# A conditional adapter with layer norm and a per-sample projection: transposes moved from TensorE to VectorE and DMA

## The reference

```python
h = relu(x @ W1[id0] + b1)                 # 512 -> 128
a = x + (h @ W2[id0] + b2)                 # 128 -> 512
n = (a - mean(a)) * rsqrt(var(a) + 1e-5)   # over the 512 columns
x1 = x + n * gamma + beta
out = x1 + (x1 @ W[id1] + b)               # 512 -> 512
```

## Time and profile before

| what | value |
|---|---|
| median of 3 runs (lowest, highest) | 313.99 us (313.78, 314.19) |
| span of the profiled execution | 312.3 us |
| PE busy | 303.9 us (97%) |
| DVE, ACT, POOL busy | 225.6, 211.1, 225.8 us (72%, 68%, 72%) |
| TensorE clock granted | 1.00 of full speed in every slice |
| DMA packets, volume | 40943 packets, 65.39 MB |

### The profile page before, as it was taken

One profiled execution on the slowest core, in us unless ns is written; L12 is line 12 of the kernel. 1 busy time (PEld: TensorE's weight loads), 2 busy tenths in 40 slices (PEclk: granted clock), 3 DMA queues, 4 the chain that ended last, 5 costly groups with the idle time before them and its releaser, 6 DMA issues.

```text
span 312.3 us, 4810 instructions
## 1 busy us (share of the span) xinstructions
PE 303.9 (97%) x1424; PEld 244.4 (78%) x1424; DVE 225.6 (72%) x641; ACT 211.1 (68%) x381; POOL 225.8 (72%) x185
## 2 busy tenths in 40 slices
PE   8988999999999999999999999999999999999995
PEld 8424678888888888888888888888888888888884
DVE  0185989696986869598686969778695977889610
ACT  1045667886696958778596857958686874857431
POOL 0649685999779995999959996899959995541000
PEclk9999999999999999999999999999999999999999
DMA  6999795778766798768867888677867381111122
GB/s 199 338 364 370 237 338 176 218 233 284 216 172 212 207 297 250 182 185 258 275 192 197 232 256 247 154 215 246 303 202 198 111 300 37 67 67 71 67 101 101
DMA packets 40943, 65.39 MB, mean 209 GB/s; under 512 B 6100, under 2 KB 10196, under 8 KB 40916
## 3 DMA queue, kind: packets, MB, share of 16 engines
q1 hardware_dynamic: 40336, 64.03, 66.2%
q10 hardware_dynamic: 580, 1.05, 1.1%
HBM read 48.29 MB, written 16.78 MB: 208 GB/s over the span
## 4 chain that ended last, share of the span: by engine, by line
PE 92%; DVE 4%; ACT 2%; issue 1%; POOL 0%; POOLq 0%
PE out_ps L778 54%; PE down_ps L778 14%; PE h_ps L778 13%; PE turn_ps L833 9%; PE turn_ps L904 2%; DVE y L488 1%; ACT y L376 1%; DVE stats L493 1%; DVE turn_ps L532 0%; DVE x1T_lo L539 0%; ACT w_hi L347 0%; ACT hT L358 0%; ACT out_sb L394 0%; DVE mean_var L497 0%; ACT w_hi L341 0%
## 5 line engine op out<-in xcount | busy, mean ns | idle before, releaser
L778 PE MATMUL out_ps<-x1T_hi,w_hi 128*128 128x512 f32 x256 | 100.4, 392 | 0.0
L778 PE MATMUL out_ps<-x1T_lo,w_hi 128*128 128x512 f32 x256 | 99.8, 390 | 0.0
L778 PE MATMUL out_ps<-x1T_hi,w_lo 128*128 128x512 f32 x256 | 99.7, 389 | 0.0
L687 POOL TENSOR_TENSOR xrow<-xrow,b_rows 128x512 f32<-128x512 f32 x64 | 82.6, 1294 | 9.3 <-DMA xrow<-x_rows 9.3
L385 ACT ACTIVATE x1T_hi<-turn_ps,gamma_beta 128x512 fp32r<-128x512 f32 x64 | 43.2, 689 | 43.7 <-DVE turn_ps L532 43.7
L532 DVE SCALAR_TENSOR_TENSOR turn_ps<-turn_ps,gamma_beta,xT 128x512 f32<-128x512 f32 x64 | 45.4, 754 | 34.4 <-PE turn_ps L833 33.5
L376 ACT ACTIVATE y<-y,shift,rstd 128x512 f32<-128x512 f32 x64 | 52.2, 818 | 20.4 <-DVE shift L523 20.0
L692 POOL TENSOR_TENSOR xT_lo<-xT,xT_hi 128x512 fp32r<-128x512 f32 x48 | 62.4, 1300 | 4.7 <-ACT xT_hi L328 4.7
L488 DVE TENSOR_TENSOR y<-down_ps,xrow 128x512 f32<-128x512 f32 x64 | 43.7, 683 | 19.6 <-PE down_ps L778 19.5
L778 PEld LDWEIGHTS out_ps<-x1T_hi,w_hi 128*128 128x128 f32 x256 | 48.1, 188 | 10.9 <-issue 0.8
L778 PEld LDWEIGHTS out_ps<-x1T_hi,w_lo 128*128 128x128 f32 x256 | 48.1, 188 | 10.1 <-issue 0.2
(11 more groups left out here) (40 smaller groups left out, 356.8 us busy)
## 6 DMA issues: line engine op xcount, KB each, us to landing
xrow<-x_rows SPq DMA_DIRECT2D x32, 512.0 KB, 6.7
out_cols<-out_sb SPq DMA_DIRECT2D x64, 256.0 KB, 2.6
xT<-x_cols SPq DMA_DIRECT2D x30, 512.0 KB, 6.2
w<-w_all SPq DMA_DIRECT2D x8, 1024.0 KB, 7.2
w<-w_all SPq DMA_DIRECT2D x15, 256.0 KB, 5.2
b_rows<-b_all SPq DMA_DIRECT2D x8, 256.0 KB, 8.1
xT<-x_cols ACTq DMA_DIRECT2D x4, 256.0 KB, 4.6
w<-w_all SPq DMA_DIRECT2D x4, 64.0 KB, 3.7
```

The source lines that it names most:

```text
L687: nc.gpsimd.tensor_tensor(xrow[:, i % XR, :], xrow[:, i % XR, :], b2_rows[:, m % 2, :], ALU.add).then_inc(rowbias_done, 1)
L778: mm = nc.tensor.matmul(out, lhsT, rhs, start=first and n == 0, stop=last and n == len(terms) - 1)
```

## The change

From tile 8 on (block 2; `SQUARED` is 8) `turn` is gone. In its place `square(i)` on VectorE transposes each 32x32 square of a normalised tile into an SBUF tensor `squares`, and `move(blk)` copies these to their places in `normT` by 16 DMAs of 64 KB a block, in rows of 512 bytes, eight issued by SP and eight by ScalarE. `merge` reads `normT` instead of PSUM. For this the rows of a block are loaded in another order (row 4p+t of the block in partition p of tile t), and `relu` writes its block in that order.

From tile 11 on (`POWER`) GpSimd takes the inverse root as a power (`inverse_root`), after an `add_eps` on VectorE; `standard` and the Newton step are gone there. `up` is one float32 product for every tile, so `x_hi`, `x_lo`, `w1_high` and `w1_low` are gone. Merges come two steps later (s modulo 4 is 3 or 0), `out(s)` becomes `out(s-9)` with steps 13 and 15 left without one, `finish` and `store` follow it, and the columns are loaded 8 tiles ahead instead of 10.

```diff
-    LOAD_COLS, LOAD_ROWS = 10, 6
-    OUT = -7
+    LOAD_COLS, LOAD_ROWS = 8, 6
+    OUT = -9
+    SQUARED = 2 * BLOCK
+    POWER = OPEN = 11
+    def merged(s):
+        first = {3: s - 7, 0: s - 6}.get(s % BLOCK, -1)
+        return (first, first + 1) if first >= SQUARED and there(first) else ()
+    def out_of(s):
+        i = {7: 0, 8: 1, 9: 2, 10: 3, 11: 4, 12: 5, 13: -1, 14: 6, 15: -1, 16: 7}.get(s, s + OUT)
+        return i if there(i) else None
+    def moved(s):
+        blk = (s - 5) // BLOCK
+        return blk if s % BLOCK == 1 and SQUARED <= blk * BLOCK < TILES else None
...
+            def move(blk):                                   # ScalarE; SP has range(2)
+                act.wait_ge(square_done, BLOCK * (blk + 1) - SQUARED)
+                act.wait_ge(merge_done, BLOCK * blk)
+                for q in range(2, KC):
+                    for j in range(KC):
+                        source = squares[Q * q:Q * (q + 1), blk % 2].rearrange("a (k j) r -> a k j r", j=KC)[:, :, j, :]
+                        nc.scalar.dma_start(normT[Q * j:Q * (j + 1), :, q * P:(q + 1) * P], source
+                                            ).then_inc(moved_in[q], 16)
...
             def step(s):                                     # ScalarE
+                if out_of(s - 1) is not None:
+                    finish(out_of(s - 1))
+                if moved(s) is not None:
+                    move(moved(s))
+                if there(s + NORM):
+                    normalise(s + NORM)
                 if (s + UP) % BLOCK == BLOCK - 1 and there(s + UP):
                     relu((s + UP) // BLOCK)
+                for i in merged(s):
+                    x1_high(i)
                 if (s + UP) % BLOCK == BLOCK - 1 and there(s + UP):
                     h_high((s + UP) // BLOCK)
...
+            def square(i):                                   # VectorE
+                blk, t = i // BLOCK, i % BLOCK
+                dve.wait_ge(norm_done, i + 1)
+                nc.vector.transpose(squares[:, blk % 2, :, t::BLOCK], y[:, i % WR, :]).then_inc(square_done, 1)
             def step(s):                                     # VectorE
+                if there(normed):
+                    mean_shift(normed)
+                if there(new):
+                    add_rows(new)
+                if first is not None:
+                    merge(first)
+                if there(new):
+                    statistics(new)
+                if second is not None:
+                    merge(second)
+                if there(new):
+                    mean_variance(new)
+                if first is not None:
+                    x1_low(first)
+                if there(new):
+                    add_eps(new)
+                if second is not None:
+                    x1_low(second)
+                if there(normed):
+                    square(normed)
...
+            def inverse_root(i):                             # GpSimd, last in its step(s)
+                pool.wait_ge(vareps_done, i - POWER + 1)
+                nc.gpsimd.tensor_tensor(rstd[:, r], var_eps[:, r], neg_half[:], ALU.pow).then_inc(rstd_done, 1)
...
-                for i in turned(s):                          # TensorE
-                    turn(i)
                 if there(s + DOWN):
                     down(s + DOWN)
                 if there(s + UP):
                     up(s + UP)
```

More of the change, by code:

```diff
@@ L84, in cond_resid_kernel @@
         y = sb("y", [P, WR, D])
+        squares = sb("squares", [P, 2, D // Q, P])
+        normT = sb("normT", [P, KC, NB])
         x1T_hi = sb("x1T_hi", [P, WR, NB], f32r)
@@ L136, in cond_resid_kernel @@
         up_done, down_done, turn_done, out_done = (sem(n) for n in ("up_done", "down_done", "turn_done", "out_done"))
-        xhi_done, xlo_done = sem("xhi_done"), sem("xlo_done")
+        square_done = sem("square_done")
+        moved_in = [sem(f"moved_in{q}") for q in range(KC)]
         relu_done, hhi_done, hlo_done = sem("relu_done"), sem("hhi_done"), sem("hlo_done")
@@ L241, in load_rows @@
                     sp.wait_ge(y_done, i + 2 - XR)
-                sp.dma_start(xrow[:, i % XR:i % XR + 2, :],
-                             x_rows[i * P:(i + 2) * P, :].rearrange("(t p) d -> p t d", p=P)
-                             ).then_inc(rows_in[i // 2 % (XR // 2)], 16)
+                if i < SQUARED:
+                    rows = x_rows[i * P:(i + 2) * P, :].rearrange("(t p) d -> p t d", p=P)
+                else:
+                    first, t = i - i % BLOCK, i % BLOCK
+                    rows = x_rows[first * P:first * P + NB, :].rearrange("(p t) d -> p t d", t=BLOCK)[:, t:t + 2, :]
+                sp.dma_start(xrow[:, i % XR:i % XR + 2, :], rows).then_inc(rows_in[i // 2 % (XR // 2)], 16)
             def store(i):
@@ L300, in step @@
                     load_b(s // PER)
-                if there(s + FINISH):
-                    store(s + FINISH)
+                if s >= 8 and out_of(s - 1) is not None:
+                    store(out_of(s - 1))
             opening()
@@ L395, in finish, with move @@
                                      bias=b[:, i // PER, i % KC:i % KC + 1]).then_inc(final_done, 1)
+            def move(blk):
+                act.wait_ge(square_done, BLOCK * (blk + 1) - SQUARED)
+                act.wait_ge(merge_done, BLOCK * blk)
+                for q in range(2, KC):
+                    for j in range(KC):
+                        source = squares[Q * q:Q * (q + 1), blk % 2].rearrange("a (k j) r -> a k j r", j=KC)[:, :, j, :]
+                        nc.scalar.dma_start(normT[Q * j:Q * (j + 1), :, q * P:(q + 1) * P], source
+                                            ).then_inc(moved_in[q], 16)
             def opening():
@@ L433, in opening @@
                 finish(1)
-                x_hi(16)
                 x1_high(4)
@@ L450, in step @@
             def step(s):
-                for i in turned(s):
-                    x1_high(i)
-                if there(s + FINISH):
-                    finish(s + FINISH)
+                if out_of(s - 1) is not None:
+                    finish(out_of(s - 1))
+                if moved(s) is not None:
+                    move(moved(s))
+                if there(s + NORM):
+                    normalise(s + NORM)
                 if (s + UP) % BLOCK == BLOCK - 1 and there(s + UP):
                     relu((s + UP) // BLOCK)
-                if there(s + XHI):
-                    x_hi(s + XHI)
+                for i in merged(s):
+                    x1_high(i)
                 if (s + UP) % BLOCK == BLOCK - 1 and there(s + UP):
                     h_high((s + UP) // BLOCK)
-                if there(s + NORM):
-                    normalise(s + NORM)
                 m, part = s // PER, s % PER
-                if part == 0 and m + 1 < SAMPLES:
-                    w1_high(m + 1)
                 if part == 4 and m + 1 < SAMPLES:
@@ L470, in step @@
                     w_high(m, k)
-                if there(s + DOWN):
-                    standard(s + DOWN)
             opening()
@@ L512, in rstd_newton, with add_eps @@
                                         ALU.mult, ALU.mult).then_inc(newton_done, 1)
+            def add_eps(i):
+                r = slice(i % WR, i % WR + 1)
+                dve.wait_ge(mean_var_done, i + 1)
+                nc.vector.tensor_scalar(var_eps[:, r], mean_var[:, i % WR, 1:2], EPS, None, ALU.add
+                                        ).then_inc(vareps_done, 1)
             def rstd_end(i):
@@ L633, in opening @@
                 x1_low(7)
+                square(8)
+                square(9)
             def step(s):
[L636 to L669, removed]
+                normed, new, first, second = s + NORM, s + DOWN, *(merged(s) or (None, None))
@@ new lines, in step @@
+                if there(normed) and normed < POWER:
+                    rstd_start(normed)
+                    rstd_newton(normed)
+                    rstd_end(normed)
+                if there(normed):
[8 more added lines that the diff above has]
+                    merge(second)
@@ L767, in step @@
                     w_low(m, k)
+                if there(s):
+                    inverse_root(s)
+            nc.gpsimd.memset(neg_half[:], -0.5).then_inc(half_done, 1)
+            pool.wait_ge(half_done, 1)
             pool.wait_ge(ident_done, 1)
@@ L783, in up @@
                 k, blk, m = i % KC, i // BLOCK, i // PER
[L784 to L793, removed]
+                wait_cols(pe, i)
+                if i < KC:
+                    pe.wait_ge(w1_first_in[k], 16)
+                if i % PER == 0 and m >= 1:
+                    pe.wait_ge(w1_in[m % 2], 16 * ((m + 1) // 2))
                 if k == 0 and blk >= 2:
                     pe.wait_ge(relu_done, blk - 1)
[L796 to L801, removed]
+                product(h_ps[blk % 2][:], [(w1[:, m % 2, k], xT[:, i % XC, :])], first=k == 0, last=k == KC - 1
+                        ).then_inc(up_done, 1)
```

(4 more changed lines are left out.)

87 lines of the change are left out of this document (35 added, 52 removed).

## The result

| what | before | after |
|---|---|---|
| median (lowest, highest), n | 313.88 us (313.39, 314.19), 4 | 398.83 us (398.70, 399.19), 4 |
| ratio, 95% | | 1.2714 [1.2688, 1.2739] |
| span of the profiled execution | 312.3 us | 396.9 us |

The account below looks back on a forecast made before the run. TensorE bound the kernel before; after the change, a VectorE-ScalarE-GpSimd series would. Shift 17 at 86.3, five turns of 41.28 to 292.7, last steps to 322.6, tail to 339.5, final `out` and end to 353.8, plus 1.7: 355 us; range 318 to 380.

Parts of the forecast that it names:

- TensorE's share: TensorE: `turn` removed 24.4 us, plain `up` adds 8.6 and `out` 1.9; net -13.9, a step 4.30 us.
- The ring: VectorE, ScalarE, GpSimd and back run in series each step, shift to shift: 41.28 us per eight steps, 36.2 before.
- the prices: Costs taken for each new operation, such as square 0.69, GpSimd's power 0.30 and ScalarE's DMA issue 0.45 us.
- 0.45 for each of ScalarE's eight: ScalarE's queue: each of its eight DMA issues a block takes 0.45 us, 3.6 in which it computes nothing.
- `square`, to the issues or to the next shift: VectorE's transpose: lasts 0.69 us, next start after 0.60, like other operations of its size.
- power to shift, start to start: GpSimd's inverse root to VectorE's `mean_shift`: 0.30 us for the power plus 0.05 for the semaphore, 0.35.
- The bounds: Unknown prices at their ends: total 338 us at the lowest, 384 with a power of 1.29, about 375 with dear squares.
- The 375 for a square of 1.4: VectorE: if a square takes 1.4 us, six of eight steps lose at most 0.8 each; total about 375.
- Rival 2: VectorE's merge and GpSimd's `bias_rows` exclude each other: merge waits 0.53 in three steps, 9 us, total 364; chance 0.15.
- Rival 3: Dear small things: power near 1.29, landings near 9.3, or issues stalling on a full queue; 370 to 385 us; chance 0.13.
- Rival 1: TensorE stays the bound, the series fitting in 4.3 us a step on average; 302 us; chance 0.15.
- Rival 4: Half coupled: ScalarE's issues overlap its computing and `w_low` gets ahead; 315 to 335 us; chance 0.12.

Follow-up runs that it names:

- the last experiment: Changed kernel with GpSimd's power first, ScalarE's eight DMAs left out, squares written densely and `bias_rows` on one column: 313.27 us, 0.999 of the kernel before.

## Why the prediction was right in direction and half in size

**TensorE's share** held: the undisturbed steps of the last experiment are 4.30, and plain `up` costs 10.2 us for the 10.5 taken.

**The ring** held, in path and in place. The shifts after start at 206.25, 212.90, 217.10, 222.50, 227.53, 234.96, 240.38, 246.53 and 253.92, steps 5, 6, 7, 0, 1, 2, 3, 4. Measured and, in brackets, predicted: 6.65 (4.65), 4.20 (4.01), 5.40 (4.81), 5.03 (4.81), 7.43 (5.19), 5.42 (5.26), 6.15 (5.65), 7.39 (6.90). The sum is 47.67 instead of 41.28. In steps 5 and 1, which begin with the issues, lie 4.2 of the 6.4 us by which it is longer.

**The step that failed is the prices**, every unknown one on the same side:

| term | taken | measured | in a turn |
|---|---|---|---|
| "0.45 for each of ScalarE's eight" | 3.6 | 5.2 (0.65 each) | 2 x 1.6 = 3.2 |
| `square`, to the issues or to the next shift | 0.60 | 1.05 or 0.94 | 2 x 0.45 + 2 x 0.34 = 1.6 |
| power to shift, start to start | 0.35 | 0.59 | 5 x 0.24 = 1.2 |
| merge beside `bias_rows`, start to start | 0.67 | 0.96 | 3 x 0.30 = 0.9 |

The sum, 6.9, stands against 6.4 seen. The four squares are those of the chain from 206.25 to 253.92: one before each round of issues, one in step 7 and one at the end of step 1. The sizes agree with the experiments: 5.75 turns x 1.6 = 9 (9.7 measured), and 5.75 x 0.9 = 5 for the exclusion (4.6).

From shift 17 to shift 57 five turns take 331.65 - 91.83 = 239.8 instead of 206.4: 33.4 of the 43.1 us between the spans. The opening is 5.5 late (91.83, predicted 86.3), and the rest, 4.2, is in the last steps. The end's issues (4.8) and landing (2.24) are together no longer than taken (3.6 + 3.7).

**The bounds** failed with them. The upper end came from one price at a time, and for the issue I let be an upper bound though no row there has a DMA from SBUF to SBUF with rows of 512 bytes. The trace of before did hold dearer issues, which I left out. The loads of b2's rows occupied SP for 0.79 us in the median (ns, least, median and longest):

```profile
L217 SPq DMA_DIRECT2D b_rows<-b_all x8: 333/794/1874, 4.6 to 216.8; - x8
```

Where no row shows an operation, the rows chosen can all lie on one side of it. The 375 for a square of 1.4 is not worked out either: at 0.8 each, four squares a turn give 373 and six 383. The square's upper bound, 1.4, did hold the truth; the value chosen, "all operations of its size last 0.68 to 0.75", holds for a dense write only.

**Rival 2** (the lock) was right and should have been a term. The wait is the 0.49 from the merge's start to `bias_rows`' end; a merge ends 0.55 after it instead of 0.74 after its own start, which leaves 0.30 of the 0.53 that I had. The Trainium skill (SBUF — State Buffer, Who interferes with whom) has the two exclude each other. This trace agrees, except that the merge ends only 0.55 us after the other and not a whole 0.74. **Rival 3** was right that the issues are dear; the power (0.55) and the landings (median 2.1) were not near its 1.29 and 9.3, and the 398.83 us lie above its 370 to 385. **Rival 1** would not have given 302 but 313: the last experiment is nearest to that case. In its profiled execution (span 313.8) TensorE stands still for 17.8 us instead of 8.4, of which 3.7 lie between 61 and 95 us and 8.0 behind 260, and it is busy for 296.0 instead of 303.9 - 13.9 = 290.0, in part at a lower clock. Its first 61 us cost what they did before. **Rival 4** did not occur: ScalarE computes nothing while it issues (the row of 5.17 us above).

**TensorE's clock** was no term of mine, and is none of the sum. In five turns the granted clock was 0.92:

```profile
61.00:332.00 271.00, 213.61 (x757) 153.63 (x756) 183.96 (x361) 118.81 (x182) 137.85 (x137) 0.92 0.72 209
```

It fell where TensorE had stood still. After the standstill of 5.14 us before 203.43 the first matmuls start 0.43 apart, and from 206.56 on 0.23: the levels of 1.2 and 2.4 GHz. While the ring sets the pace this should cost little, since TensorE holds 8% of the chain; no run isolates it. A repair that leaves short standstills pays for it: in the last experiment the twelve products at 95.28, behind a standstill of 1.92 us, are on the chain and take 4.60 us instead of 2.77.

## What to carry to other kernels

When work leaves the busiest engine, first draw the order of what is left as a ring: from an instruction of a step back to itself one step later, with every engine that it passes. If that ring is longer than the busiest engine's step, the work saved there is worth nothing; the last link (here a power of 0.55 us behind 2.5 us of unrelated work) decides, and moving it was worth 32 us. Count DMA issues as work of the engine that makes them, with a price measured for that very pattern, or else between the cheapest and the dearest row of the trace, and price a rearranging write by its step and not by its size.

## What the runs showed of the hardware

- Issuing a DMA of 64 KB from SBUF to SBUF in rows of 512 bytes occupies an engine's queue for 0.65 us (in the changed kernel 0.59 at the least and 0.62 in the median, at most 1.22, and 0.03 to the next). SP and ScalarE take the same, and so does SP when it issues alone; ScalarE was not run alone. 64 KB loads took 0.33 to 0.40. Its landing took 2.0 to 3.7 us in the changed kernel, up to 7.6 with the issues in two fours.
- A VectorE transpose of 32x32 squares, 128x512 float32, lasts 0.70 us with a dense write and 1.11 with a step of 16 bytes.
- GpSimd's power on 128x1 lasts 0.55 us; a memset of this shape took 0.10.
- VectorE's merge of two SBUF tensors ends 0.55 to 0.57 us after a GpSimd 128x512 instruction that was running when it began: 1.04 us in the changed kernel, up to 1.70 with the power first, 0.74 alone. A GpSimd one that begins beside a running merge takes 1.73 to 1.76 instead of 1.29. In a few cases GpSimd's next instruction goes first as well; the longest merge, with the power first and ScalarE's DMAs out, lasts 2.27.
